# A hybrid layer on one core: the time mix's output product as three products of high parts and rests, with a new order of all engines' work

## The chip, the cores and the metric

The kernel runs on one core of a Trainium2 chip. A core has a matrix engine (TensorE, PE in the profile, with its weight loads as PEld), VectorE (DVE), ScalarE (ACT), GpSimd (POOL) and the queue of SyncE (SP), which issues most transfers. The metric is the device time of the program in microseconds (us). Lower is better.

## The reference, cut to what matters

The input x has 16 sequences of 512 tokens with 256 features. Four layers are added to it one after the other: a time mix with a channel mix, a layer of experts, a gated recurrence, and the same experts again. The part that the change touches is the time mix:

```
xn = layer_norm(x, ln1_w, ln1_b)
lx = time_shift(xn)
k = (xn * time_mix_k + lx * (1.0 - time_mix_k)) @ w_key      # v and r alike
out = wkv(w, time_first, k, v)                                # a recurrence over the tokens
x = x + out * sigmoid(r) @ w_output                           # this product changes
xn2 = layer_norm(x, ln2_w, ln2_b)                             # the channel mix follows
x = x + sigmoid(fr) * (square(relu(fk)) @ f_w_value)
```

and the last lines of the gated recurrence, `out = out @ W_out.T`, `rms = rsqrt(mean(out * out) + EPS)` and `out * rms * gamma`. The experts work on the first two sequences only (1024 tokens, two experts of eight for each token).

## The kernel before

One sequence is one run b of the time and channel mix (16 runs); the gated recurrence has runs p in an order of its own (`ORDER`), and the experts work on 20 tiles of 128 token rows in each of their two rounds (tiles 0 to 19 and 20 to 39). For each engine the order of the work is written out by hand: functions `turn_first`, `turn_0` to `turn_16` list calls such as `keys(5)` or `tile_up(8, 0)`, and each called helper waits on the semaphores of what it needs. Nothing is reordered when the program runs, so a helper that waits holds all that stands behind it on its engine. Turn i is about run i of the time mix, run i - 1 of the channel mix, and, from turn 4 on, a run of the recurrence and some tiles of the experts. The second round of the experts begins in turn 11 and needs the recurrence of the first two sequences, which are its runs 5 and 6.

A run of the time mix goes like this. Tokens are rows of a tile at first; TensorE transposes them (`transposes_in`), ScalarE writes the normed columns into `xn`, VectorE makes the differences and three mixed inputs. Keys, values and receptances are products of the weights `kw` with those inputs. They are split already: each float32 factor is written as a high part in the type float32r and the rest (also float32r), and `columns_split` adds three products, high by high, high by rest and rest by high. ScalarE makes a high part with a copy (`high_of_key`, L1240), VectorE the rest with a subtraction (`low_of_key`, L3372). Then VectorE runs the recurrence (`weights_ahead` to `numerators`), and `gated` ends it with the multiplication at L3480, which writes `mixed`, a half of the tile `dec`.

`outputs` on TensorE waits for that step, `mixture` "out", and multiplies `mixed` by `wo` with the helper `rows`: for each of four groups of 128 tokens and each of two groups of features one matmul with 128 columns of `mixed` as the stationary operand and 256 columns of `wo` as the moving one, in plain float32 (L2305). The trace shows a float32 matmul as two records and a float32r matmul as one. The result lies in the PSUM banks `rows_t`; `residual_mid` on VectorE (L3485) adds it to `y`, the second norm follows (`second_stats`, on GpSimd `norm2`), and `transposes_mid` on TensorE begins the channel mix. `second_differences` waits for the product too, since it writes over `dec`.

The tiles `timely` and `halves` lie at the same place in memory, one seen as float32 and one as float32r. `keys_out` on ScalarE (L1254) writes the keys into `kc`, a piece of `timely`, where `den`, the divisor of the run before, has been. The recurrence's own output product (`rec_products`, weights `gwo`) and the channel mix's receptance (`receptances`, weights `fwr`) use `rows` too, and stay as they are. Behind `rec_products` ScalarE squares the rows into a tile `square` that nobody reads, for their sum (L1364). At the start SyncE loads all weights; the ones that are split go to the tile `space`, which the recurrence uses later, and ScalarE and VectorE write the parts from there. `routing_masks` on GpSimd and `routing_spread`, `routing_counts`, `routing_products` and `slot_products` on TensorE, with small steps on VectorE between them, work out which token goes to which expert.

## Time and profile before

| | |
|---|---|
| median of 3 runs | 1272.68 us (1270.85 to 1278.52) |
| profiled execution | 1270.85 us |
| its span, first to last instruction | 1269.0 us |
| PE busy | 1173.5 us, 92% |
| DVE busy | 904.6 us, 71% |
| ACT busy | 769.0 us, 61% |
| POOL busy | 546.8 us, 43% |
| mean granted clock of TensorE | 0.975 |

Busy times are those of the profiled execution. Matmuls are pipelined, so the duration of a single matmul record is longer than the distance to the next one; what a group costs is read from the start of the group to the start of what follows. The granted clock is the share of TensorE's full speed that the chip allowed.

### The profile page before, as it was taken

How to read it: one execution, taken by the hardware profiler on the slowest of the kernel's cores; microseconds unless marked ns; L12 is line 12 of the kernel's file. 1: busy time of each engine (PE TensorE's matmuls, PEld its weight loads, DVE VectorE, ACT ScalarE, POOL GpSimd, SP SyncE). 2: the span in 40 equal slices, each digit the busy share in tenths (PEclk: the TensorE clock that was granted, in tenths of full speed). 3: DMA queues.
4: the chain of work that ended last, by engine and by line, in shares of the span. 5: the costliest groups of instructions: out<-in, count | busy, mean ns of one | idle time of the engine just before them, and what ended most of it. 6: DMA issues, size and time to landing. Idle time of an engine off the chain costs nothing. (4 is left out here: it accounts for less than half of the span.)

```text
span 1269.0 us, 17607 instructions
## 1 busy us (share of the span) xinstructions
PE 1173.5 (92%) x5992; PEld 968.4 (76%) x5992; DVE 904.6 (71%) x1539; ACT 769.0 (61%) x1164; POOL 546.8 (43%) x533
## 2 busy tenths in 40 slices
PE   4599999999999999999988999999999999998982
PEld 2487778888887877788876878878878788787871
DVE  7898887657666767776889898677686847544244
ACT  3464565754756657666757777568566575563533
POOL 3436742635034332362676546634453604323024
PEclk9699999999999999999999999999999999999996
DMA  7102156738556474574442134774667646756444
GB/s 207 31 18 50 18 146 202 209 96 221 181 160 189 115 209 130 162 216 157 109 91 59 26 67 140 205 203 134 161 163 201 170 149 179 216 162 140 130 151 123
DMA packets 115624, 180.64 MB, mean 142 GB/s; under 512 B 10312, under 2 KB 86736, under 8 KB 115536
## 3 DMA queue, kind: packets, MB, share of 16 engines
q1 hardware_dynamic: 94720, 124.46, 30.6%
q0 software_dynamic: 15056, 49.83, 19.9%
q10 hardware_dynamic: 5760, 5.25, 1.2%
q8 instruction: 48, 0.79, 0.3%
q14 instruction: 40, 0.33, 0.1%
HBM read 140.16 MB, written 16.27 MB: 123 GB/s over the span
## 5 line engine op out<-in xcount | busy, mean ns | idle before, releaser
L2394 PE MATMUL psum<-fwv,hid 128*128 128x256 f32 x1024 | 238.2, 382 | 3.8 <-ACT hid L1290 3.7
L2394 PEld LDWEIGHTS psum<-fwv,hid 128*128 128x128 f32 x1024 | 191.5, 191 | 31.1 <-ACT hid L1290 4.9
L803 POOL TENSOR_TENSOR rstd<-varis,half_neg 128x4 f32<-128x4 f32 x64 | 87.8, 1372 | 247.1 <-DVE varis L3316 180.1
L2435 PEld LDWEIGHTS psum<-xst,ew 128*128 128x128 f32 x1024 | 123.9, 193 | 5.8 <-ACT xst L1371 1.1
L2435 PE MATMUL psum<-xst,ew 128*128 128x128 f32 x1024 | 126.2, 277 | 1.1 <-DMA ew<-in_w 0.6
L2443 PE MATMUL psum<-ew,hidt 128*128 128x256 f32 x512 | 116.0, 380 | 1.3 <-ACT hidt L1384 1.3
L2443 PEld LDWEIGHTS psum<-ew,hidt 128*128 128x128 f32 x512 | 96.7, 190 | 15.3 <-ACT hidt L1384 1.9
L1286 ACT ACTIVATE hid<-psum 128x512 f32<-128x512 f32 x128 | 74.8, 594 | 54.9 <-PE psum L2298 34.8
L1384 ACT ACTIVATE hidt<-psum 128x512 f32<-128x512 f32 x80 | 47.9, 599 | 94.0 <-PE psum L2435 78.7
L927 POOL DMA_INDIRECT xs<-xf_rows,token_of_slot x40 | 52.8, 1320 | 119.4 <-PE psum L2423 102.7
L2298 PE MATMUL psum<-halves,kw_hi 128*128 128x512 f32 x360 | 103.7, 410 | 0.5 <-ACT timely L1259 0.4
L807 POOL TENSOR_SCALAR xhat<-rows_ring,negmean,rstd 128x256 f32<-128x256 f32 x104 | 97.4, 947 | 11.9 <-PE psum L2287 5.7
L2298 PE MATMUL psum<-xfk_hi,fwk_hi 128*128 128x512 f32 x256 | 90.0, 433 | 2.2 <-DVE parts L3337 1.5
L2298 PEld LDWEIGHTS psum<-halves,kw_hi 128*128 128x128 f32 x360 | 66.6, 191 | 19.0 <-issue 2.4
L2298 PE MATMUL psum<-xfk_hi,fwk_lo 128*128 128x512 f32 x256 | 81.0, 398 | 0.0
L2298 PE MATMUL psum<-parts,fwk_hi 128*128 128x512 f32 x256 | 80.6, 396 | 0.0
L1290 ACT ACTIVATE hid<-hid 128x512 f32<-128x512 f32 x128 | 78.1, 628 | 2.7 <-ACT ys L1392 1.6
L2298 PE MATMUL psum<-parts,gw_hi 128*128 128x512 f32 x256 | 72.2, 405 | 7.9 <-ACT space L1327 4.1
L2287 PE MATMUL psum<-ident,xhat 128*128 128x128 f32 x360 | 50.2, 285 | 30.9 <-POOL xhat L807 14.1
L3535 DVE SCALAR_TENSOR_TENSOR space<-space,vec 128x512 f32<-128x512 f32 x90 | 62.4, 760 | 14.3 <-ACT space L1307 14.3
L2287 PEld LDWEIGHTS psum<-ident,xhat 128*128 128x128 f32 x360 | 42.7, 147 | 38.0 <-issue 20.0
L3372 DVE TENSOR_TENSOR halves<-timely,halves 128x1024 fp32r<-128x1024 f32 x45 | 56.9, 1273 | 20.5 <-ACT halves L1248 7.8
(334 smaller groups left out, 2594.8 us busy)
## 6 DMA issues: line engine op xcount, KB each, us to landing
ew<-in_w SPq DMA_DIRECT2D x64, 1024.0 KB, 5.9
ew<-in_w SPq DMA_DIRECT2D x64, 512.0 KB, 5.1
rows_ring<-bias_rows POOLq DMA_DIRECT2D x28, 512.0 KB, 5.6
rows_ring<-in_x SPq DMA_DIRECT2D x14, 512.0 KB, 5.5
rows_ring<-y POOLq DMA_DIRECT2D x14, 512.0 KB, 6.1
out<-rows_ring SPq DMA_DIRECT2D x14, 512.0 KB, 7.1
rows_ring<-sf POOLq DMA_DIRECT2D x13, 512.0 KB, 6.3
rows_ring<-space POOLq DMA_DIRECT2D x12, 512.0 KB, 6.5
```

The source lines that it names most:

```text
L803: pool.tensor_tensor(dst, src, half_neg[:, 0:src.shape[1]], ALU.pow).then_inc(done, 1)
L807: pool.tensor_scalar(dst[:, c, :], src[:, c, :], negmean[n][:, c:c + 1], rstd[n][:, col0 + c:col0 + c + 1], ALU.add, ALU.mult).then_inc(st ...
L927: pool.indirect_dma_start(out=xs[n % 2][:], out_offset=None, in_=xf_rows, in_offset=bass.IndirectOffsetOnAxis(ap=token_of_slot[:, t:t + 1] ...
L1286: nc.scalar.activation(hid[:, j % NHID, :], ring[f"f{j}"], ACT.Relu).then_inc(relu.sem, 1)
L1290: nc.scalar.activation(hid[:, j % NHID, :], hid[:, j % NHID, :], ACT.Square).then_inc(sq.sem, 1)
L2287: last = nc.tensor.transpose(bank_t[:, c, k * P:(k + 1) * P], src[:, k, c * P:(c + 1) * P], ident[:])
L2298: last = nc.tensor.matmul(dst, w[a][:, c, m * P:(m + 1) * P], src[b][:, c, :], start=n == 0, stop=n == len(terms) - 1)
L2394: last = nc.tensor.matmul(rows4[:, k, :], hid[:, j % NHID, k * P:(k + 1) * P], fwv[:, j, :], start=j == 0 and k % 2 == 0, stop=j == FC - 1 ...
L2435: last = nc.tensor.matmul(bank_e[:, j * P:(j + 1) * P], ew1[:, c, at:at + P], xst[:, c, :], start=c == 0, stop=c == DC - 1)
L2443: last = nc.tensor.matmul(bank_e[:, 0:D], hidt[:, j, :], ew2[:, j, :], start=j == 0, stop=j == FC - 1)
L3372: nc.vector.tensor_tensor(parts[1], whole, parts[0].bitcast(F32), ALU.subtract).then_inc(lo.sem, 1)
L3535: nc.vector.scalar_tensor_tensor(s.cv[:, c, :], s.xc[:, c, j:j + T], col(f"conv{j}", c), s.cv[:, c, :], ALU.mult, ALU.add).then_inc(conv.s ...
```

## The change

The weight `wo` becomes two tiles, `wo[0]` (half of w_output as float32r) and `wo[1]` (the rest); w_output is loaded into a piece of `space` that is free then. After `gated`, ScalarE copies `mixed` to a float32r high part (`high_of_mixture`), which lies where `kc` and `den` are, and VectorE subtracts it from `mixed` in place (`low_of_mixture`). `outputs` waits for that rest and calls `rows_split`: for each group of 128 tokens six float32r matmuls instead of two float32 ones. Because the high part lies in `kc`'s place, `keys_out` now waits for the output product of the run before instead of for its `mixture`. The squares of the norm are written over the first 256 columns of the recurrence's states, which the product has read by then, and the tile `square` is gone. The calls in the turns of all five engines are in another order, and ScalarE's turns load the tables of its functions 94 times instead of 92. Cut to its core (in the turns only a few are shown, with the engine behind their first line):

```diff
...
-        wo = sb("wo", [P, DC, D])
+        wo = [sb(f"wo_{part}", [P, DC, D], F32R) for part in ("hi", "lo")]
...
+        with nc.sbuf_tensor("dec_parts", [P, 2, DC, T], F32R) as dec_parts:
+            mixed_parts = [carved(halves, 3 * DC * T, DC, T), dec_parts[:, 1]]
...
+        wo_whole = space[:, DC * FF + 5 * DC * D:DC * FF + 6 * DC * D].rearrange("p (c n) -> p c n", c=DC)
...
-        square = sb("square", [P, D])
...
+        mixture_hi = steps("mixture_hi", ["hi"], B)
+        mixture_lo = steps("mixture_lo", ["lo"], B)
+        wo_split = sem("wo_split")
...
-            for dst, src in ((wo, w_output), (fwr, f_w_recept), (fwv, f_w_value), (gwo, w_out_t)):
+            load_weight(wo_whole, w_output, weights_loaded)
+            for dst, src in ((fwr, f_w_recept), (fwv, f_w_value), (gwo, w_out_t)):
...
+            def high_of_mixture(b):
+                act.wait_ge(mixture.sem, mixture.count(b, "out"))
+                nc.scalar.activation(mixed_parts[0], mixed, ACT.Copy).then_inc(mixture_hi.sem, 1)
+
...
-                await_step(act, mixture, b - 1, "out")
+                await_step(act, proj, b - 1, "o")
...
-                    nc.scalar.activation(square[:], rows_t[:, c, :], ACT.Square, accum_out=ssq[:, c:c + 1])\
+                    nc.scalar.activation(rec_sets[set_of(p)].hs[:, 0, 0:D], rows_t[:, c, :], ACT.Square, accum_out=ssq[:, c:c + 1])\
...
+            def rows_split(dst, src, w, st):
+                terms = [(c, a, b) for a, b in ((0, 0), (1, 0), (0, 1)) for c in range(DC)]
+                for k in range(TC):
+                    for n, (c, a, b) in enumerate(terms):
+                        last = nc.tensor.matmul(dst[:, k, :], src[b][:, c, k * P:(k + 1) * P], w[a][:, c, :], start=n == 0,
+                                                stop=n == len(terms) - 1)
+                last.then_inc(st.sem, 1)
+
...
-                    pe.wait_ge(split_his, 3)
+                    pe.wait_ge(wo_split, 1)
...
-                pe.wait_ge(mixture.sem, mixture.count(b, "out"))
-                rows(rows_t, mixed, wo, DC, proj)
+                pe.wait_ge(mixture_lo.sem, mixture_lo.count(b, "lo"))
+                rows_split(rows_t, mixed_parts, wo, proj)
...
+
+            def split_wo_low():
+                dve.wait_ge(split_his, 3)
+                nc.vector.scalar_tensor_tensor(wo[1][:], wo_whole, 0.5, wo[0][:].bitcast(F32), ALU.mult, ALU.subtract)\
+                    .then_inc(wo_split, 1)
+
+            def low_of_mixture(b):
+                dve.wait_ge(mixture_hi.sem, mixture_hi.count(b, "hi"))
+                nc.vector.tensor_tensor(mixed_parts[1], mixed, mixed_parts[0].bitcast(F32), ALU.subtract).then_inc(mixture_lo.sem, 1)
...
-                nc.scalar.mul(wo[:], wo[:], 0.5).then_inc(split_his, 1)
+                nc.scalar.activation(wo[0][:], wo_whole, ACT.Copy, scale=0.5).then_inc(split_his, 1)
...
             def turn_0():   # TensorE
-                routing_spread()
                 freed(ev2, -1, 'e1')
                 freed(fr_out, -1, 's')
                 transposes_in(1)
                 freed(ev1, 1, 'e1')
                 outputs(0)
-                keys(1)
-                routing_counts()
-                routing_products()
                 freed(zsum, 0, 'z')
                 transposes_mid(0)
+                keys(1)
                 value_columns(1)
+                recept_columns(1)
+                channel_key(0, 0)
+                channel_key(0, 1)
...
             def turn_first():   # GpSimd
-                routing_masks()
                 norm1(0)
                 decay_power()
                 keep1(0)
+                norm1(1)
...
             def turn_0():   # GpSimd
-                norm1(1)
+                keep2(0)
                 norm2(0)
-                keep2(0)
+                routing_masks()
                 keep1(1)
...
             def turn_15():   # VectorE
-                weights_ahead(15)
                 gated_values(13)
-                surpluses(15)
-                low_of_receptance(15)
                 second_differences(14)
                 channel_mix_key(14)
+                low_of_receptance(15)
                 channel_mix_high(14)
+                channel_mix_receptance(14)
+                surpluses(15)
+                recur(12)
                 channel_mix_low(14)
-                channel_mix_receptance(14)
+                weights_decayed(15)
                 third_stats(13)
+                weights_now(15)
                 mean_square(12)
                 finish(12)
-                weights_now(15)
+                beta_sums(15)
+                decayed_values(15)
                 taps(13)
                 split_taps(13)
-                weights_decayed(15)
-                beta_sums(15)
-                denominators(15)
-                decayed_values(15)
                 alpha_sums(15)
                 weighted_values(15)
+                gated_input(13)
                 numerators(15)
+                denominators(15)
                 gated(15)
-                dve.wait_ge(mixture.sem, mixture.count(B - 1, 'out'))
-                nc.vector.memset(rec_sets[1].xc[:, :, 0:3], 0.0).then_inc(cols_made, 1)
+                low_of_mixture(15)
                 scales(13)
-                gated_input(13)
                 residual_mid(15)
+                second_stats(15)
...
```

The list of calls moves as a whole, so three places are shown as the engines' rows. The first is TensorE from its first instruction to the products of run 1 (`ident,xhat` is a transposition of tokens, `timely,space` the three unsplit products of run 0, `ew` with few columns the routing). Before:

```order
L2287 MATMUL psum<-ident,xhat 128x128 x8
L2292 MATMUL psum<-timely,space 128x512 x12
L2485 MATMUL psum<-ew 128x128 x2
L2486 MATMUL psum<-ew 128x1
L2287 MATMUL psum<-ident,xhat 128x128 x8
L2305 MATMUL psum<-wo,dec 128x256 x8
L2298 MATMUL psum<-halves,kw_hi 128x512 x4
```

and with the change:

```order
L2315 MATMUL psum<-ident,xhat 128x128 x8
L2320 MATMUL psum<-timely,space 128x512 x12
L2315 MATMUL psum<-ident,xhat 128x128 x8
L2341 MATMUL psum<-wo_hi,halves 128x256 x2
L2341 MATMUL psum<-wo_lo,halves 128x256 x2
L2341 MATMUL psum<-wo_hi,dec_parts 128x256 x2
...
L2315 MATMUL psum<-ident,xhat 128x128 x8
L2326 MATMUL psum<-halves,kw_hi 128x512 x4
```

The output product grows from 8 to 24 matmuls (the three rows stand four times, once for each group of tokens), the routing's first products are gone from here, and the transposition for run 0's channel mix now stands ahead of run 1's keys.

The second place is VectorE at the end of run 15 of the time mix. `dec<-timely,dec` ends `gated`, `y<-psum,y` is `residual_mid`, and the rows on `space` belong to the recurrence's run 13. Before:

```order
L3477 SCALAR_TENSOR_TENSOR timely<-timely 128x1024
L3480 TENSOR_TENSOR dec<-timely,dec 128x1024
L4274 MEMSET timely 128x2x3
L3554 TENSOR_TENSOR space<-space 128x1024
L3556 TENSOR_SCALAR space<-space 128x1024
L3678 SCALAR_TENSOR_TENSOR space<-space 128x1024
L3485 TENSOR_TENSOR y<-psum,y 128x1024
```

and with the change:

```order
L3522 SCALAR_TENSOR_TENSOR timely<-timely 128x1024
L3525 TENSOR_TENSOR dec<-timely,dec 128x1024
L3426 TENSOR_TENSOR dec_parts<-dec,halves 128x1024
L3599 TENSOR_TENSOR space<-space 128x1024
L3601 TENSOR_SCALAR space<-space 128x1024
L3530 TENSOR_TENSOR y<-psum,y 128x1024
```

The new subtraction stands right behind the multiplication whose result it needs, with ScalarE's copy between the two.

The third place is TensorE near the end: from the last part of run 14's channel mix (`fwv,hid`) to the transposition for the recurrence's run 14 (`ident,y`). Before:

```order
L2394 MATMUL psum<-fwv,hid 128x256 x8
L2435 MATMUL psum<-xst,ew 128x128 x8
L2305 MATMUL psum<-gwo,space 128x256 x8
L2298 MATMUL psum<-xfk_hi,fwk_hi 128x512 x2
...
L2423 MATMUL psum<-ident,xs 128x128 x2
L2287 MATMUL psum<-ident,y 128x128 x8
```

and with the change:

```order
L2430 MATMUL psum<-fwv,hid 128x256 x8
L2315 MATMUL psum<-ident,xhat 128x128 x8
L2471 MATMUL psum<-xst,ew 128x128 x8
L2333 MATMUL psum<-gwo,space 128x256 x8
L2471 MATMUL psum<-xst,ew 128x128 x8
...
L2459 MATMUL psum<-ident,xs 128x128 x2
L2430 MATMUL psum<-fwv,hid 128x256 x4
L2315 MATMUL psum<-ident,y 128x128 x8
```

Between the two ends there now stand another transposition (`transposes_mid(15)`), one more half tile of the experts (`xst,ew`) and one more part of the channel mix (`fwv,hid` x4), and four key products (`xfk_hi,fwk_hi` with their two companions) instead of five.

## Rows read from the trace of the kernel before

**Rows 1.** Stretches of the span, all engines: length, then busy time of each
```profile
core 0: us, PE busy (x) PEld busy (x) DVE busy (x) ACT busy (x) POOL busy (x), PEclk, DMA share, GB/s
40.00:60.00 20.00, 13.44 (x49) 11.15 (x50) 16.36 (x38) 6.92 (x8) 3.61 (x3) 0.67 0.05 10
60.00:200.00 140.00, 133.76 (x626) 112.30 (x626) 121.81 (x209) 80.69 (x110) 70.86 (x62) 0.97 0.30 75
200.00:600.00 400.00, 393.64 (x2132) 326.42 (x2132) 276.26 (x449) 251.80 (x377) 153.63 (x157) 1.00 0.60 169
600.00:760.00 160.00, 147.48 (x679) 122.00 (x678) 141.42 (x256) 111.83 (x169) 100.58 (x85) 0.98 0.33 74
760.00:1160.00 400.00, 393.27 (x2105) 324.01 (x2104) 273.11 (x437) 255.83 (x404) 168.09 (x155) 1.00 0.62 174
1160.00:1218.00 58.00, 53.41 (x272) 46.73 (x271) 19.84 (x42) 27.41 (x48) 11.11 (x15) 0.97 0.40 108
```
**Rows 2.** Timeline of PE around 604 us: start, us, line, operation, count
```profile
603.34 1.09 PE L2298 MATMUL psum<-halves,kw_hi 128*128 128x512 f32 x4
604.26 0.62 PE L2298 MATMUL psum<-halves,kw_lo 128*128 128x512 f32 x2
604.72 1.95 PE L2435 MATMUL psum<-xst,ew 128*128 128x128 f32 x16
606.51 3.62 PE L2305 MATMUL psum<-gwo,space 128*128 128x256 f32 x16
609.96 1.95 PE L2435 MATMUL psum<-xst,ew 128*128 128x128 f32 x16
```
**Rows 3.** Timelines of PE and, last, DVE at the start
```profile
41.57 1.97 PE L2287 MATMUL psum<-ident,xhat 128*128 128x128 f32 x8 [11.89 <-POOL xhat L807]
45.08 6.63 PE L2305 MATMUL psum<-wo,dec 128*128 128x256 f32 x16 [1.54 <-ACT xn L1220]
51.35 1.27 PE L2298 MATMUL psum<-halves,kw_hi 128*128 128x512 f32 x4
54.30 0.28 PE L2490 MATMUL psum<-ew 128*128 128x1 f32 x2
59.80 1.94 PE L2287 MATMUL psum<-ident,xhat 128*128 128x128 f32 x8 [0.81 <-DVE xhat L3508]
...
41.21 1.38 DVE L3480 TENSOR_TENSOR dec<-timely,dec 128x1024 f32<-128x1024 f32 x1
```
**Rows 4.** Groups of VectorE and ScalarE: count | busy, mean ns | idle before
```profile
L3372 DVE TENSOR_TENSOR halves<-timely,halves 128x1024 fp32r<-128x1024 f32 x45 | 56.9, 1273 | 20.5 <-ACT halves L1248 7.8 <-ACT halves L1240 7.2 <-ACT halves L1244 5.4
L1240 ACT ACTIVATE halves<-timely 128x1024 fp32r<-128x1024 f32 x15 | 15.8, 1052 | 9.2 <-DVE timely L3329 9.2
```
**Rows 5.** Timelines of DVE and PE, runs 3, 11 and 15
```profile
194.47 1.22 DVE L3480 TENSOR_TENSOR dec<-timely,dec 128x1024 f32<-128x1024 f32 x1
195.84 3.69 PE L2305 MATMUL psum<-wo,dec 128*128 128x256 f32 x16
...
791.79 3.69 PE L2305 MATMUL psum<-wo,dec 128*128 128x256 f32 x16 [0.17 <-DVE dec L3480]
...
1127.71 1.22 DVE L3480 TENSOR_TENSOR dec<-timely,dec 128x1024 f32<-128x1024 f32 x1
1130.26 3.62 PE L2305 MATMUL psum<-wo,dec 128*128 128x256 f32 x16
```
**Rows 6.** GpSimd: its norm rows, durations min/median/max, and four of them at 31.81
```profile
L807 POOL TENSOR_SCALAR xhat<-rows_ring,negmean,rstd x104: 543/554/3556, 80.0 to 1217.7; 128x256 f32<-128x256 f32 x104
...
31.81 9.71 POOL L807 TENSOR_SCALAR xhat<-xf,negmean,rstd 128x256 f32<-128x256 f32 x4 [0.20 <-issue]
```
**Rows 7.** Timeline of PE at the end of the dense part
```profile
1150.28 1.95 PE L2435 MATMUL psum<-xst,ew 128*128 128x128 f32 x16
...
1165.94 0.38 PE L2423 MATMUL psum<-ident,xs 128*128 128x128 f32 x2
1170.90 1.94 PE L2287 MATMUL psum<-ident,y 128*128 128x128 f32 x8 [4.59 <-DVE space L3578]
```

More of the change, by code:

```diff
@@ L1610, in turn_5 @@
[L1610 to L1623 removed]
+                relu_of(4, 5)
@@ L1762, in turn_8 @@
-            def turn_8():
                 rows_back(15)
                 tile_columns(16)
+            def turn_8():
+                norm_mid(7)
+                high_of_value(8)
+                high_of_receptance(8)
+                keys_out(8)
                 values_out(8)
+                nc.scalar.preload_act_table_set(GELU_TANH)
+                receptances_out(8)
                 rows_of_two(16, 0)
+                sums_of_squares(3)
+                relu_of(7, 0)
                 rows_of_two(16, 1)
+                square_of(7, 0)
@@ L1805, in turn_8 @@
                 gelu_of(18, 0)
+                high_of_key(9)
+                high_of_receptance(9)
                 gelu_of(18, 1)
+                rows_back(18)
                 relu_of(7, 5)
-                nc.scalar.preload_act_table_set(LOG_EXP)
-                root_of(4)
-                rows_back(18)
+                relu_of(7, 6)
+                high_of_value(9)
+                tile_columns(19)
+                keys_out(9)
+                gelu_of(19, 0)
+                square_of(7, 4)
@@ L2724, in turn_5 @@
+                channel_key(4, 7, 1)
+                tile_up(8, 1)
                 channel_value(4, 4)
-                keys(6)
-                channel_value(4, 5)
-                tile_down(9)
+                tile_down(8)
                 freed(zsum, 5, 'z')
                 transposes_mid(5)
-                tile_in(10)
+                tile_in(9)
+                keys(6)
+                value_columns(6)
+                tile_up(9, 0)
+                channel_value(4, 5)
                 channel_value(4, 6)
@@ L4124, in turn_11 @@
                 mixed_receptance(12)
+                gated_values(10)
+                residual_mid(11)
+                low_of_key(12)
                 second_stats(11)
```

1969 lines of the change are left out of this document (991 added, 978 removed).

## The prediction, made before the changed kernel was run

> **What bounds the kernel now.** I read the stretches of the span first. From 200 to 600 us and from 760 to 1160 us TensorE is busy for 393.6 and 393.3 of 400 us while VectorE is busy for 276 and 273 [rows 1]: there each microsecond of matrix work is one of the program. From 60 to 200 us TensorE idles 6.2 of 140 us with VectorE 87% busy (121.8), and from 600 to 760 us it idles 12.5 of 160 us with VectorE 88% busy (141.4) [rows 1]: there both engines are nearly full, and the chain through VectorE has a say. Second comes the timeline of TensorE, for what a matmul costs: the reader is to take start to start. 16 records of plain float32 with 256 moving columns take 609.96 - 606.51 = 3.45 us, 216 ns each; 16 records with 128 moving columns take 606.51 - 604.72 = 1.79 us, 112 ns each; six float32r matmuls with 512 columns take 604.72 - 603.34 = 1.38 us, 230 ns each [rows 2]. Third, the start and the end, where TensorE waits: for 11.89 us before 41.57 [rows 3], and for 4.59 us before 1170.90 [rows 7]. Fourth, how far the output product stands behind the multiplication that feeds it. In run 3 the one ends at 195.69 and the other starts at 195.84, in run 15 the distance is 1.33 us, and in run 11 the product waited 0.17 us [rows 5].
>
> **Matrix work of the product.** In each of 15 runs the 16 records of 3.45 us are replaced by 24 float32r ones with 256 moving columns. No such row exists. The nearest from below is 112 ns: a record with a weight load of the same size that streams half as long [rows 2]. If the time of a float32r matmul goes with its columns, 256 of them take half of 230 ns, 115; if the 14 ns by which it exceeds the float32 record (230 - 216) are a fixed price of each matmul, it is 216 / 2 + 14 = 122 ns. I take 118, between these two. 24 x 118 = 2.83 us, 0.62 less than 3.45, and 15 x 0.62 = 9.3 us. Run 0 goes at a granted clock of 0.67 and its product takes 51.35 - 45.08 = 6.27 us [rows 1, 3]; in the same ratio (2.83 / 3.45) it is 1.1 us less. Term: -10.4. Its ends: 112 ns give 15 x 0.76 + 1.4 = -12.8; 122 ns give 15 x 0.52 + 0.9 = -8.7; the upper end of what the rows allow is 230 ns, if the weight load and not the streaming sets the pace of float32r, and it is a rival below. The Trainium skill, page "TensorE: Matmul & The Clock Gate", section "Back-to-back issue gap", has columns / 2.4 + 2.5 ns, 109 ns for 256 columns; this term by it would be -14.0. For the 512 columns of float32r here it gives 216 ns where the row has 230, so the row decides.
>
> **VectorE's new subtraction.** One for each run, 16 in all, at 1273 ns for the same form and size [rows 4], 20.4 us, and 0.7 us once for the weight's rest. Where TensorE is the bound, VectorE's idle third covers it: nothing. In runs 1 to 3 and in 9 and 10, which fall into the two stretches where VectorE is 87 to 88% busy [rows 1], there is little cover. There I give back the matrix saving, 5 x 0.62 = 3.1 us, and count half of the new work, 5 x 1.27 / 2 = 3.2. Term: +6.3. Ends: 0 (the saving is kept and the idle eighth covers it) and 3.1 + 6.4 = +9.5. GpSimd may feel it as well: four norm rows of GpSimd took 9.71 us at 31.81 where one is 554 ns in the median and up to 3556 [rows 6], beside VectorE's work. The Trainium skill, "GPSIMD Engine Reference", section "1. Specifications", says that GpSimd shares its SBUF interface with VectorE instructions that have two SBUF inputs; the new subtraction is one, and by that rule each would hold GpSimd for its length, which speaks against the change: 16 x 1.27 = 20.4 us of GpSimd's time would go by it. GpSimd is busy 153.6 of 400 us and 100.6 of 160 [rows 1], so it has room for delays of that size, and I add nothing.
>
> **ScalarE's copy and two more table loads.** 16 x 1.05 us at the row of the same copy [rows 4], under 20 us with the tables, on an engine busy 252 and 256 of 400 us in the dense stretches [rows 1]. Cover: its idle third. Nothing, and at most what the next term has. The later release of `keys_out` costs nothing either, since it also waits for the keys' own product, which stands behind the output product on TensorE. The squares go to another place at the same size; w_output is one transfer of the same size to another place.
>
> **The wait for the rest.** From the multiplication to the product there are now ScalarE's copy, 1.05 us, VectorE's subtraction, 1.27, and handoffs, about 2.5 us. At the old distances runs 3, 10 and 11 (0.15 us each) would be short by 2.35 and runs 1 and 15 (about 1.3) by 1.2: 3 x 2.35 + 2 x 1.2 = 9.5 us [rows 5] (they show 3, 11 and 15 of the sixteen pairs in the timelines). Behind the waiting product stand the experts' tiles and, through `residual_mid`, the second norm. The new order was made with this step in it: in VectorE's rows of run 15 nothing stands between the multiplication and the subtraction. I take +1, with ends 0 and +9.5.
>
> **The start.** The norm rows of run 1 and their transposition move ahead, so the 11.89 us of waiting go; but the output product of run 0 still ends a chain on VectorE that ends at 42.59 (41.21 + 1.38) and now has copy and subtraction behind it: it starts at 42.59 + 2.5 = 45.1, as now at 45.08 [rows 3]. It is 1.1 us shorter (counted above). The dense part begins with run 0's second transposition, 59.80 now, and some 2 us earlier then, since the routing's small steps are gone from VectorE in front of it. But the keys' products of run 1, 54.30 - 51.35 = 2.95 us, and the routing's own matmuls, about 2 us, which filled the gap, go behind it. 2.95 + 2 - 2 - 1.1 = +1.9, and I take +1.5. Ends: -1 and +4.
>
> **The end.** In front of the transposition that waited 4.59 us stood 1165.94 - 1150.28 = 15.7 us of other work [rows 7]. Now it is one transposition (8 records of 112 ns, 0.9 us), one half tile (1.79) and one part of the channel mix (8 records of 216 ns, 1.7) more, and one key product (six of 230 ns, 1.4) less: 3.0 us more cover for the same chain. I take -2; ends -4.6 and +2. Behind it the recurrence's last run is the same work in the same order.
>
> **Sum:** -10.4 + 6.3 + 1 + 1.5 - 2 = -3.6, from 1270.85 for the profiled execution (span 1269.0 and 1.85 around it) to 1267.2. The median of before, 1272.68, is 1.8 us above that execution. I say 1267. One per cent, 12.7 us, is about what this measurement can tell from no change: the bounds are 1260.0 and 1285.4. The likeliest case's own range is 1261 to 1275, chance 0.50.
>
> **Rivals.** (1) The saving arrives whole and the new order closes gaps. TensorE idled 36 us between 60 and 1218 us [rows 1] (6.2 + 6.4 + 12.5 + 6.7 + 4.6); if a quarter of that goes as well, it is -10.4 - 9 = -19, 1252. For it: the lists were redone on all engines. Against: the idle time is largest where VectorE is full, and VectorE gets 21 us more. Chance 0.30. (2) The rest comes too late. The high part and the rest are two new steps in a row, and where the product stands closer than 2.5 us behind the multiplication TensorE stands still, in the two stretches where VectorE is full also for the steps behind it: -10.4 + 9.5 + 9.5 + 4 = +12.6, 1283. It decides as soon as the distances of rows 5 are kept in the runs named. Chance 0.14. (3) Float32r is paced by its weight loads: then 24 x 230 ns = 5.52 us instead of 3.45, 15 x 2.07 = +31.1 and run 0 +3.8; nothing is left to give back, so with the new work, the wait, the start and the end (3.2 + 1 + 1.5 - 2) it is 1270.85 + 38.6 = 1309. The point from which the product itself loses is 3.45 / 24 = 144 ns. For it: every float32r row that there is has 230 ns. Against: a float32 record with its load of 128 columns comes each 112 ns [rows 2]. Chance 0.06.
>
> **Range and chances.** Low end: -12.8 with no loss elsewhere and part of rival 1, 1252. High end: rival 2 with the product at 122 ns, 1286. What is outside is rival 3 and the tails, under 2 in 10. Faster by over 1%: most of rival 1 and a little of the main case, 0.30. Slower by over 1%: rival 3 and near half of rival 2, 0.12. Within: 0.58.
>
> **What would show it.** The output product from start to the next start: 2.83 us (2.7 to 2.95), not 5.5. TensorE's wait in front of it, by release from the subtraction: under 2 us in sum, against 9.5 in rival 2. Idle time of TensorE from 600 to 760 us: above 12.5 us here, below it in rival 1. TensorE's dense part begins near 57.7 us, and the wait in front of the last-but-one transposition of the recurrence is under 3 us. Wrong it would be if the new order moved TensorE's idle time by more than 10 us either way, which no row of the kernel before can tell.

## The result, and the profile after

The changed kernel takes 1255.03 us (median of 4 runs, 1253.22 to 1259.97), the kernel before, timed beside it, 1273.82 (1270.85 to 1278.52): a ratio of 0.9855, 95% interval 0.9813 to 0.9897, some 18.8 us less. Run again with the experiments it took 1253.01 against 1274.79, a ratio of 0.9838 (0.9818 to 0.9859). The forecast was 1267 in a range of 1252 to 1286, with 0.58 on "within 1%" and 0.30 on faster. The time is in the range, but the kernel is faster by over 1%, which had 0.30: it is the time of rival 1, outside the main case's own 1261 to 1275.

The page of the changed kernel, busy time of each engine (before: 1173.5, 904.6, 769.0 and 546.8 us in a span of 1269.0):

```profile
span 1252.9 us, 17899 instructions
PE 1159.5 (93%) x6120; PEld 963.1 (77%) x6120; DVE 927.4 (74%) x1556; ACT 786.5 (63%) x1182; POOL 586.9 (47%) x533
```

The stretches of the span, with the same columns as [rows 1]; the bounds are moved with the work:

```profile
40.00:60.00 20.00, 6.04 (x31) 5.90 (x32) 18.04 (x29) 4.01 (x4) 7.83 (x17) 0.59 0.14 26
60.00:200.00 140.00, 135.75 (x681) 115.24 (x679) 123.86 (x219) 90.60 (x120) 85.63 (x67) 0.98 0.28 69
200.00:600.00 400.00, 396.17 (x2209) 330.11 (x2208) 290.93 (x465) 259.49 (x387) 176.99 (x161) 1.00 0.62 175
600.00:745.00 145.00, 132.59 (x612) 109.81 (x611) 129.64 (x223) 100.17 (x152) 92.34 (x78) 0.95 0.30 67
745.00:1140.00 395.00, 389.00 (x2123) 322.11 (x2123) 280.15 (x461) 262.95 (x407) 178.43 (x155) 1.00 0.62 173
1140.00:1202.00 62.00, 61.22 (x328) 53.60 (x328) 28.41 (x52) 31.93 (x59) 12.32 (x14) 1.00 0.51 136
1202.00:1252.90 50.90, 22.97 (x109) 18.45 (x107) 24.56 (x41) 16.90 (x34) 20.88 (x22) 0.77 0.48 143
```

Read length minus busy time of PE. From 60 us to the end of the dense part TensorE idles 4.3, 3.8, 12.4, 6.0 and 0.8 us, 27.3 together, where [rows 1] give 36.4. VectorE is 23 us busier, and TensorE still waits less. From 600 to 760 us it idles 12.4 us, as before (12.5). The prediction had wanted more in its main case and less in rival 1, so this sign decides nothing.

The timeline of TensorE at run 1's output product and the next group, then at run 0's product and the start of the dense part:

```profile
92.88 0.58 PE L2341 MATMUL psum<-wo_hi,halves 128*128 128x256 f32 x2
93.30 0.40 PE L2341 MATMUL psum<-wo_lo,halves 128*128 128x256 f32 x2
...
95.66 0.40 PE L2341 MATMUL psum<-wo_hi,dec_parts 128*128 128x256 f32 x2
95.90 1.46 PE L2430 MATMUL psum<-fwv,hid 128*128 128x256 f32 x6
...
44.98 0.77 PE L2341 MATMUL psum<-wo_hi,halves 128*128 128x256 f32 x2 [15.00 <-DVE dec_parts L3426]
45.97 0.63 PE L2341 MATMUL psum<-wo_hi,dec_parts 128*128 128x256 f32 x2
...
49.16 0.40 PE L2341 MATMUL psum<-wo_hi,dec_parts 128*128 128x256 f32 x2
58.53 1.94 PE L2315 MATMUL psum<-ident,xhat 128*128 128x128 f32 x8 [8.97 <-DVE xhat L3553]
```

From the second pair of records to the next group there are 22 records in 95.90 - 93.30 = 2.60 us, 118 ns each: the price that was taken. The first pair takes 93.30 - 92.88 = 0.42 us, though, so the whole product lasts 3.02 us here. In the 14 runs in which the next group follows at once it lasts 2.90 to 3.04 us, 2.92 in the median, instead of the 2.83 that were forecast. The dense part begins at 58.53 instead of 59.80. And the end of the dense part, against the wait of 4.59 us in [rows 7]:

```profile
1156.83 0.38 PE L2459 MATMUL psum<-ident,xs 128*128 128x128 f32 x2
1157.05 1.89 PE L2430 MATMUL psum<-fwv,hid 128*128 128x256 f32 x8
1158.78 1.04 PE L2315 MATMUL psum<-ident,y 128*128 128x128 f32 x8
```

The wait is gone. Behind the last tile of the experts the program takes 48.0 us where it took 50.0 (1252.9 - 1204.9 and 1269.0 - 1219.0). The matmuls there are the same and run at a higher granted clock (the gates' products take 5.7 us at 1.00 instead of 7.3 at 0.79), and the new order alone has 50.1, so these 2 us are not the order's.

What TensorE waited for in the changed kernel (the waiting line, the step that released it, sum in us, times, longest), and the new steps' groups (count | busy, mean ns | idle before and what ended it):

```profile
PE psum L2333 <- DVE space L3608: 21.2, 5, 11.7
PE psum L2315 <- DVE xhat L3553: 18.7, 2, 9.8
PE psum L2341 <- DVE dec_parts L3426: 16.2, 4, 15.0
PE psum L2315 <- POOL xhat L813: 3.6, 2, 2.5
...
L3426 DVE TENSOR_TENSOR dec_parts<-dec,halves 128x1024 fp32r<-128x1024 f32 x16 | 19.8, 1238 | 18.5 <-ACT halves L1258 18.5
L1258 ACT ACTIVATE halves<-dec 128x1024 fp32r<-128x1024 f32 x16 | 16.9, 1056 | 8.2 <-DVE dec L3525 7.8 <-ACT ys L1402 0.4
```

The wait for the rest is 16.2 us, but 15.0 of them are the start, where TensorE has no other work; in the other runs of the time mix it is 1.2. The groups show another wait: VectorE stands idle 18.5 us in front of its subtraction, because ScalarE's copy comes late, up to 5.51 us late:

```profile
411.25 1.23 DVE L3525 TENSOR_TENSOR dec<-timely,dec 128x1024 f32<-128x1024 f32 x1
417.98 1.23 DVE L3426 TENSOR_TENSOR dec_parts<-dec,halves 128x1024 fp32r<-128x1024 f32 x1 [5.51 <-ACT halves L1258]
```

So the result looks like rival 1: the whole saving and 9 us of idle time (36.4 - 27.3). The experiments say otherwise.

### The profile page after: what moved, and what is told of

Read it like the earlier page. It is cut to its first block, busy times and chain, and to the rows that moved or that the text cites. A ratio compares the mean times of both kernels' runs of the same rounds, so it can differ in the third digit from the quotient of the medians.

```text
span 1252.9 us, 17899 instructions
## 1 busy us (share of the span) xinstructions
PE 1159.5 (93%) x6120; PEld 963.1 (77%) x6120; DVE 927.4 (74%) x1556; ACT 786.5 (63%) x1182; POOL 586.9 (47%) x533
## 4 chain that ended last, share of the span: by engine, by line
PE 24%; DVE 9%; issue 7%; ACT 4%; POOL 4%; DMA 2%; DVEq 0%; POOLq 0%; ACTq 0%
PE psum L2326 8%; PE psum L2333 4%; PE psum L2430 4%; PE psum L2471 2%; PE psum L2479 2%; DVE space L3580 1%; PE psum L2493 1%; PE psum L2511 1%; PE psum L2315 1%; DVE stats L3345 1%; POOL xhat L813 1%; DMA rows_ring<-sf 1%; POOL rstd L809 1%; DVE timely L3365 1%; DVE dec L3377 1%
## 5 line engine op out<-in xcount | busy, mean ns | idle before, releaser
L809 POOL TENSOR_TENSOR rstd<-varis,half_neg 128x4 f32<-128x4 f32 x64 | 99.2, 1550 | 205.7 <-DVE varis L3352 142.1
L813 POOL TENSOR_SCALAR xhat<-rows_ring,negmean,rstd 128x256 f32<-128x256 f32 x104 | 116.7, 1132 | 10.5 <-POOL rstd L809 5.8
L2333 PE MATMUL psum<-gwo,space 128*128 128x256 f32 x240 | 62.9, 422 | 21.2 <-DVE space L3608 21.2
L2333 PEld LDWEIGHTS psum<-gwo,space 128*128 128x128 f32 x240 | 50.7, 215 | 33.1 <-issue 21.1
L1226 ACT ACTIVATE xn<-psum,vec 128x512 f32<-128x512 f32 x64 | 46.2, 775 | 45.2 <-PE psum L2315 42.3
```

The source lines that it names most:

```text
L809: pool.tensor_tensor(dst, src, half_neg[:, 0:src.shape[1]], ALU.pow).then_inc(done, 1)
L813: pool.tensor_scalar(dst[:, c, :], src[:, c, :], negmean[n][:, c:c + 1], rstd[n][:, col0 + c:col0 + c + 1], ALU.add, ALU.mult).then_inc(st ...
L2333: last = nc.tensor.matmul(dst[:, k, :], src[:, c, k * P:(k + 1) * P], w[:, c, :], start=c == 0, stop=c == chunks - 1)
```

## The experiments

Twelve runs in three groups of four, each timed beside the kernel before, whose medians in the groups were 1272.56, 1274.79 and 1274.44. Each ratio is to the kernel before of its own group. A difference between two ratios carries the noise of both: worked out from their 95% intervals it is good to about 4 us either way, and to 6 against the first measurement of the changed kernel. In the diffs, lines are against the changed kernel unless it says otherwise.

**The new order alone.** The old product, its weight and its waits, with the changed kernel's calls in their new order:

```diff
-                pe.wait_ge(mixture_lo.sem, mixture_lo.count(b, "lo"))
-                rows_split(rows_t, mixed_parts, wo, proj)
+                pe.wait_ge(mixture.sem, mixture.count(b, "out"))
+                rows(rows_t, mixed, wo, DC, proj)
...
-                high_of_mixture(0)     # and the other 15, and low_of_mixture
```

> The changed kernel's order of all engines with the old float32 product (no high part, no rest, wo in float32, keys_out waits for the mixture again). Theory A, two gains: the product's 24 records at 118 ns save 0.6 us in each run (10.4 us in all) and the new order by itself takes some 9 us of TensorE's idle time away; then this kernel is 8 to 10 us slower than the changed one, 1263 to 1266 us, and clearly faster than the kernel before. Theory B, the order only hides the new steps of ScalarE and VectorE: then the order alone brings nothing, and this kernel is at 1270 to 1275 us. Theory C, the order brings all and the product nothing: 1253 to 1257 us.

Measured: 1252.95 us, ratio 0.9848 (0.9825 to 0.9870). That is Theory C: the order alone brings 19.6 us, as much as the whole change, and the product with its steps nothing on top. (The squares keep their new place in this kernel. The third splice below has that place too and takes the time of before, so the place is worth nothing.) Its stretches:

```profile
60.00:200.00 140.00, 136.85 (x666) 116.54 (x665) 121.02 (x218) 87.10 (x116) 82.42 (x66) 0.99 0.28 69
200.00:600.00 400.00, 396.62 (x2147) 328.67 (x2146) 283.04 (x456) 253.84 (x380) 177.13 (x160) 1.00 0.62 175
600.00:745.00 145.00, 134.17 (x607) 111.03 (x607) 129.45 (x232) 100.21 (x152) 93.85 (x81) 0.96 0.30 67
745.00:1140.00 395.00, 391.32 (x2096) 324.39 (x2096) 277.30 (x450) 259.73 (x404) 178.30 (x157) 1.00 0.62 174
1140.00:1200.00 60.00, 60.00 (x318) 52.74 (x317) 24.33 (x48) 30.22 (x59) 12.42 (x16) 1.00 0.49 139
```

TensorE idles 3.2, 3.4, 10.8, 3.7 and 0 us, 21.0 together instead of 36.4: 15.4 us of the 17.9 by which the two profiled spans differ (1269.0 and 1251.1). The tail behind the last tile of the experts is as long as before (50.1 against 50.0 us). The waits that went are those of [rows 7] (4.59) and many small ones. TensorE's waits for GpSimd's norm rows (`xhat`) come to 2.7 us in 2 places where they were 14.1 in 5 (11.9 of these stood at the start, where 12.6 on the multiplication now stand instead).

**The new form in the old order.** The kernel before with the new product, the copy put behind `norm_in` of the next run, the subtraction behind the multiplication or the next `first_differences`:

```diff
...
                 norm_in(6)
+                high_of_mixture(5)
...
                 gated(5)
+                low_of_mixture(5)
```

> The new product in the order of the kernel before: ScalarE's copy stands right behind norm_in of the next run (or behind inverse, whichever is later), VectorE's subtraction right behind the next run's first differences where these follow gated, else right behind gated. Theory A: the product's 10.4 us come, and of the waits for the rest (short distances in runs 1, 3, 10, 11, 15) 4 to 10 us are lost: 1264 to 1270 us. Theory B: product and waits cancel and VectorE's 20 us cost more: 1272 to 1280 us. Theory C would have it at 1273 us, as before.

Measured: 1306.58 us, ratio 1.0259 (1.0231 to 1.0288), worse than all three theories. TensorE waited for the rest itself only 9.5 us, 4.0 of it at the start, so rival 2 is a small part of it. More comes by way of ScalarE, as the waits of TensorE and, last, of ScalarE show:

```profile
PE psum L2339 <- DVE dec_parts L3424: 9.5, 5, 4.0
PE psum L2324 <- ACT space L1337: 8.9, 5, 3.1
PE psum L2477 <- ACT hidt L1394: 6.9, 3, 5.6
PE psum L2324 <- ACT hid L1296: 6.6, 2, 5.8
PE psum L2428 <- ACT hid L1300: 5.6, 2, 3.6
...
ACT halves L1258 <- DVE dec L3523: 25.2, 9, 6.6
```

The copy that I had placed holds ScalarE for 25.2 us until the multiplication is done, and steps of ScalarE (`space`, `hidt`, `hid`) are late for TensorE: 28.0 us in the four rows, of which the kernel before has 4.1 for `space` and 3.7 for `hid` among its larger ones. That they are late because they queue behind the copy is read from the waits; no run shows it, and the second try below, where ScalarE's wait for the multiplication is 12.2 us instead of 25.2, was slower still.

**The third product left out.** High part of the mixture by the weight's rest is not computed, 16 records instead of 24:

```diff
-                terms = [(c, a, b) for a, b in ((0, 0), (1, 0), (0, 1)) for c in range(DC)]
+                terms = [(c, a, b) for a, b in ((0, 0), (0, 1)) for c in range(DC)]
```

> The changed kernel without the third product (high part by the weight's rest is left out): 16 instead of 24 records in each output product, 8 x 118 ns = 0.94 us less of TensorE in each of 16 runs, 15.1 us, and nothing else moved. If TensorE is the bound in all stages: 1240 us. If five runs lie where VectorE holds (my term of the prediction gave the saving of runs 1 to 3, 9 and 10 back): 11 x 0.94 = 10.3 us, 1245 us. If the order was fitted to the length of the product and gaps open: above 1247 us.

Measured: 1247.36 us, ratio 0.9798 (0.9778 to 0.9819). 8 records of 118 ns in 16 runs are 15.1 us of matrix work, and the ratio is 0.57 and 0.40 points below the two of the changed kernel, 7.3 and 5.1 us: 0.3 to 0.5 us for each. That is the third case, just above 1247 us, by a margin that the noise does not carry; 1245 is as possible. The trace speaks for gaps that open: measured as in the table of the next section, the matrix work is 12 to 14 us less than in the two profiles of the changed kernel, and TensorE idles 33.7 us where it idled 27.9 and 27.8.

**More work on VectorE.** Three small statistics instructions of an idle weight stand right behind each subtraction of runs 1 to 15; VectorE's busy time rises from 927.4 to 941.0 us:

```diff
+                if b:
...
+                    for c in range(3):
+                        nc.vector.bn_stats(spare[:, c, :], fwv[:, c, :]).then_inc(spare_made, 1)
```

> The changed kernel with more VectorE work right behind the new subtraction in runs 1 to 15: three statistics of 256 columns of a constant tile, some 1.2 us, 18 us in all, which nobody reads. My prediction charged half of the new VectorE work in runs 1 to 3, 9 and 10 (about 3 us) and nothing elsewhere: 1258 us. If VectorE has room everywhere: 1255 us. If VectorE's chains set the pace more often than its busy share tells: 1262 us or more.

Measured: 1260.85 us, ratio 0.9897 (0.9875 to 0.9919), 0.42 and 0.59 points above the two of the changed kernel: 5.3 and 7.5 us for 13.6 us of VectorE, 0.4 to 0.55 each. The smaller of the two is within its noise, the larger is not. Measured in the same way, TensorE idles 32.4 us here, 4.5 more than in the changed kernel. The idle quarter of VectorE does not hide the load, in a part of the program where TensorE is 98% busy (27.3 us idle of 1142).

**The changed kernel once more**, as the base of the next three.

> The changed kernel once more, on the same chip as the three other runs, as the base of their differences. Both theories: 1254 to 1256 us, a ratio of 0.985 to the kernel before.

Measured: 1253.01 us, ratio 0.9838 (0.9818 to 0.9859).

**The steps without the form.** Copy, subtraction and the wait for it are kept, the product is the old one:

```diff
-                rows_split(rows_t, mixed_parts, wo, proj)
+                rows(rows_t, mixed, wo, DC, proj)
...
-                nc.vector.tensor_tensor(mixed_parts[1], mixed, mixed_parts[0].bitcast(F32), ALU.subtract)
+                nc.vector.tensor_tensor(mixed_parts[0], mixed, mixed_parts[0].bitcast(F32), ALU.subtract)
```

> The new order with ScalarE's copy, VectorE's subtraction and the wait for it kept, but the product itself is the old one, 16 records of plain float32 on the multiplication's result (the subtraction's result goes to the copy's place and is read by nobody; the keys' output waits for it). Theory H (the new steps cost about half of what the cheaper product saves, and each side counts at 0.3 to 0.5 us per us): 1258 to 1262 us, 3 to 6 above the changed kernel, and 6 to 9 above the new order alone. Rival I (the new steps are hidden in the new order, and the new product simply brings nothing): 1252 to 1255, like the new order alone.

Measured: 1258.61 us, ratio 0.9874 (0.9853 to 0.9894), 5.6 above the changed kernel, or 4.6 by the ratios, just outside the noise: Theory H. Against the new order alone it is 3.3 us slower (0.26 points of the ratio), which is within the noise.

**The form without the steps.** 24 float32r records, no copy, no subtraction:

```diff
-                rows_split(rows_t, mixed_parts, wo, proj)
+                rows_split(rows_t, (mixed_parts[1], mixed_parts[1]), wo, proj)
...
-                nc.vector.tensor_tensor(mixed, den[:], num, ALU.mult).then_inc(mixture.sem, 1)
+                nc.vector.tensor_tensor(mixed_parts[1], den[:], num, ALU.mult).then_inc(mixture.sem, 1)
```

> The new order with 24 float32r records in the product, but without the copy and without the subtraction: the multiplication writes its result as float32r at once, and it stands for both parts (so the rest of the mixture is left out, and one of the three products is wrong). Theory H: the saving of 10.4 us counts at about half and nothing is paid, 1246 to 1249 us, 6 to 9 below the changed kernel. Rival I: the product brings nothing even without its steps, 1252 to 1255. Rival J (the saving arrives in full, since no step is new): 1241 to 1244.

Measured: 1244.84 us, ratio 0.9777 (0.9754 to 0.9800), below Theory H's range and near rival J's. Against the new order alone this is 0.71 points, 9.0 us, of the 10.4 that the sum had for it. Here the saving arrives nearly whole, within the noise.

**Splices of the two orders**, all with the old product. In the first, every engine takes the calls of the new order up to turn 4, and then those that are left in the old order; the second is its mirror image; the third has the old order up to turn 12.

> The old product; every engine takes the new order up to turn 4 and what is then left in the old order. The new order alone was 12.2 us ahead at run 5's output product, 9.2 at run 9's, 16.0 at run 14's and 18.0 at the last tile. Theory K (the gain is made where it shows, in pieces that don't depend on each other): the first piece stays, 1259 to 1263 us, and run 5's output product is 10 to 13 us earlier than before. Rival L (a lead made early is given back, because the old order's later work waits for other things, such as the experts' transfers and the recurrence's first runs): 1267 to 1272.

Measured: 1288.64 us, ratio 1.0116 (1.0097 to 1.0135), worse than both theories. Run 4's product stands 0.7 us ahead of before, run 5's 12.4 behind, and from there the distance stays between 12.4 and 15.7 to the end. What TensorE waited for between 289 and 372 us, at the seam:

```profile
PE psum L2478 <- DMA ew<-in_w: 6.5, 1, 6.5
PE psum L2311 <- DVE halves L3393: 3.3, 1, 3.3
```

The transfer of an expert's weights comes 6.5 us late there and the keys' parts 3.3. So this run prices its seam and not its pieces: inconclusive on Theory K, except that the old order behind the seam kept its old length.

> The old product; every engine takes the old order up to turn 4 and what is then left in the new order, the mirror image of the run that lost 13 us at its seam. Theory K: the part behind the seam is 6 to 9 us shorter than before, the total between 1264 and 1272 us by what the seam costs, and the distance from run 5's output product to the end shrinks by 5 us or more against the kernel before. Rival P: the seam alone decides again, 1280 or more.

Measured: 1259.66 us, ratio 0.9880 (0.9861 to 0.9899). Theory K, below its 1264 to 1272: the part from turn 5 on brings 14.8 us, three quarters of the order's gain. Its second sign failed, though. In the profiled execution (1258.5 us against 1269.0) run 5's output product is 6.6 us earlier than before and the distance from it to the end only 3.9 us shorter, where 5 or more were expected: most of what this profile shows is gained right behind the seam.

> The old product; every engine takes the old order up to turn 12 and what is then left in the new order. In the new order alone the distance from run 12's output product to the end is 9 to 11 us shorter than before. Theory K (the last part of the new order is shorter by itself): 1262 to 1267 us. Rival P (the new order's end is short only because its middle left the work in another state, or the seam costs what the end brings): 1271 or more, with waits of TensorE near 880 us.

Measured: 1272.76 us, ratio 0.9991 (0.9975 to 1.0007): the last turns of the new order bring nothing by themselves. The 4.59 us in front of the last-but-one transposition are gone there too, but run 12's product is 5.6 us late and run 13's 14.0 at the seam, and the end then recovers most of it (the last tile 4.9 behind). Rival P, with the same reserve as above: seam and end can't be told apart.

**The form alone in the old order.**

> The old order of all engines with 24 float32r records in the product, without the copy and without the subtraction (the multiplication writes its result as float32r and it stands for both parts; the rest of the mixture is left out). In the new order the same edit brought 9.0 us against the old product (a ratio of 0.9777 against 0.9848). Theory M (the form of the product is worth about as much in either order, and what the earlier run with the whole form in the old order lost, 34 us, came from where I put the two steps): 1262 to 1267 us. Rival N (the old order is tuned so closely to its own lengths that even a shorter product disturbs it): 1270 or more.

Measured: 1274.02 us, ratio 1.0004 (0.9990 to 1.0018). Rival N: the same edit that brings 9.0 us in the new order brings nothing in the old. Its trace shows places where it is given back. Run 3's product is 3.4 us ahead of before and run 5's 3.8, run 6's 1.6 ahead, run 9's 4.0 behind. The timeline of TensorE there, of this kernel and then of the kernel before:

```profile
473.83 0.60 PE L2484 MATMUL psum<-ident,hid_rows 128*128 128x128 f32 x4
478.58 1.09 PE L2297 MATMUL psum<-ident,xhat 128*128 128x128 f32 x8 [4.15 <-DVE space L3605]
```

```profile
475.31 0.60 PE L2466 MATMUL psum<-ident,hid_rows 128*128 128x128 f32 x4
478.24 1.07 PE L2287 MATMUL psum<-ident,xhat 128*128 128x128 f32 x8 [2.32 <-DVE space L3578]
```

TensorE arrives 1.5 us earlier and starts 0.3 us later, since VectorE's step of the recurrence was done no sooner. And there is a second loss, in the granted clock, again of this kernel and then of the one before:

```profile
480.00:500.00 20.00, 19.96 (x112) 15.60 (x108) 15.45 (x17) 13.83 (x19) 6.00 (x7) 0.93 0.53 152
640.00:660.00 20.00, 15.63 (x73) 13.22 (x73) 15.92 (x25) 12.31 (x19) 17.21 (x16) 0.83 0.17 46
700.00:720.00 20.00, 17.57 (x76) 14.91 (x77) 17.12 (x26) 14.80 (x21) 10.07 (x11) 0.83 0.28 53
```

```profile
480.00:500.00 20.00, 19.21 (x117) 15.72 (x114) 15.70 (x18) 14.24 (x20) 6.17 (x7) 1.00 0.51 151
640.00:660.00 20.00, 17.74 (x80) 14.88 (x80) 18.57 (x23) 13.72 (x21) 16.56 (x14) 0.91 0.20 56
700.00:720.00 20.00, 19.95 (x88) 16.65 (x87) 18.58 (x21) 15.99 (x22) 9.03 (x7) 0.93 0.11 21
```

Behind the longer waits the engine runs part of the time at 1.2 instead of 2.4 GHz.

**The form in the old order, the copy moved** to where its input was ready in the trace of the first try:

> The whole new form in the old order again, with ScalarE's copy moved in twelve of the sixteen runs by 1 to 8 calls, to about where its input came in the trace of the first try (which had ScalarE wait 25.2 us for the multiplication in nine runs and the copy 4 to 7 us late in four others). Theory M: most of the loss was this placement, 1272 to 1285 us against 1307. Rival O (two more steps in the chain cost the old order that much wherever the copy stands, since VectorE's work behind them is late): 1298 or more.

Measured: 1325.01 us, ratio 1.0401 (1.0379 to 1.0424), 18 worse than before the move. Rival O, and a miss of mine: TensorE now waited 24.6 us for the rest in 8 places, since every step behind the moved copies shifted as well. What the first trace said about where the copies should stand did not hold once they had been moved.

Of the kernels that compute the whole product none beats the new order alone (0.9848) and the changed kernel (0.9855 and 0.9838), and these two can't be told apart. The two with lower times, 0.9777 and 0.9798, leave a part of the product out.

## Why the prediction was right in its range and wrong in its reasons

The dense stretch, from 60 us to the last tile of the experts, splits into three parts when the stretches are read in steps of 20 us: TensorE's idle time, the time lost to the lower clock (1 minus the granted clock, times the length), and the rest, which is matrix work at full clock (good to 2 or 3 us).

| kernel | length | idle | clock | rest |
|---|---|---|---|---|
| before | 1159.0 | 37.0 | 9.4 | 1112.6 |
| new order alone | 1141.0 | 21.6 | 7.2 | 1112.2 |
| new order, steps, old product | 1147.2 | 23.2 | 9.2 | 1114.8 |
| new order, new product, no steps | 1132.4 | 23.7 | 4.6 | 1104.1 |
| changed kernel | 1144.9 | 27.9 | 11.4 | 1105.6 |
| changed kernel, second profile | 1141.0 | 27.8 | 6.4 | 1106.8 |
| old order, new product, no steps | 1163.6 | 44.3 | 15.4 | 1103.9 |
| old order, whole form | 1202.6 | 73.0 | 30.2 | 1099.4 |

**Matrix work: right in size.** 118 ns for a record was taken and 118 measured, but not for the first pair of a product (0.42 us instead of 0.24). With 2.92 us in the median a run saves 0.53 us instead of 0.62, 8.0 us in 15 runs where 9.3 were forecast. Run 0's product takes 4.4 us instead of 6.3, 1.9 us less and not 1.1, because the granted clock rose in its middle. All kernels with the new product have 6 to 13 us less in the last column. Rival 3 (paced by weight loads, 230 ns) is out. The Trainium skill, "TensorE: Matmul & The Clock Gate", section "Back-to-back issue gap", has a formula for the gap of an isolated matmul that gives 109 ns for 256 columns. The 118 ns of the trace do not agree with it.

**What the saving is worth: wrong as a rule.** The prediction said that in the dense stretches "each microsecond of matrix work is one of the program". It is that only if the rest of the program can follow. With the copy and the subtraction in place the cheaper product brings 5.6 us (1258.61 to 1253.01); without them 9.0; in the old order 0. In the new order the sum's own figure, 10.4 less the 3.1 given back, stands between the first two; it has no place for the third.

**VectorE's subtraction: the step that was mis-sized.** I charged 3.2 us, for five runs, and for the other ten nothing under "VectorE's idle third covers it". The load added on VectorE cost 0.4 to 0.55 us per us with TensorE 98% busy around it: 5.3 to 7.5 us for 13.6, where my rule (half, in five runs of fifteen) gives 2.3. The two steps together cost 8.2 us with the new product (1244.84 to 1253.01), against the 3.2 + 1 that the sum had for them and their wait. With the old product they cost 3.3, which the runs can't tell from nothing. By the lengths in the table the steps cost 8.6 us with the new product and 6.2 with the old one; the whole times show less because the two kernels without the steps had an end that was 2 us longer. A part of that is ScalarE's copy, charged at zero: it is late in 7 runs of the time mix and VectorE stands still for 18.5 us. How the 8.2 divide between copy, subtraction and the later release of the keys' output was not measured.

**GpSimd: right to add nothing, though the rule holds.** The Trainium skill, "GPSIMD Engine Reference", section "1. Specifications", lets GpSimd contend with VectorE instructions that have two SBUF inputs, and by it I had counted 20.4 us of GpSimd's time for the subtractions. The trace of the changed kernel agrees with the rule: four norm rows take 2.18 us, 0.55 each, with VectorE idle beside nearly all of them, and 6.25 us, the first two of them 2.6 each, beside VectorE's instructions with two inputs. Over the whole trace the 86 norm rows that overlap no VectorE instruction take 0.55 us in the mean, and 110 that overlap one with two SBUF inputs take 1.52.

```profile
208.19 2.18 POOL L813 TENSOR_SCALAR xhat<-y,negmean,rstd 128x256 f32<-128x256 f32 x4 [0.30 <-POOL rstd L809]
214.65 1.23 DVE L3377 TENSOR_TENSOR dec<-xn 128x1024 f32<-128x1024 f32 x1 [6.34 <-ACT xn L1226]
...
397.90 6.25 POOL L813 TENSOR_SCALAR xhat<-rows_ring,negmean,rstd 128x256 f32<-128x256 f32 x4 [0.30 <-POOL rstd L809]
397.98 2.33 DVE L3506 TENSOR_TENSOR_SCAN timely<-dec 128x512 f32<-128x512 f32 x2
```

The new subtractions hardly meet such rows: 4 of GpSimd's 244 norm rows overlap one. So GpSimd is busy for 586.1 us in the new order alone and for 586.9 with the subtractions, and the 20.4 us don't show. The 40 us more than before (546.8) come with the order: the same 104 rows of `xhat` take 947 ns in the mean before, 1148 in the new order alone and 1132 in the changed kernel.

**The wait for the rest: right.** 1 us was taken, 1.2 measured outside the start. **The start:** taken at +1.5, ends -1 and +4. The dense part begins 1.3 us earlier (2 were expected), and 2.8 us earlier in the new order alone (57.05), which has no steps behind the multiplication. The work that was moved into it is as expected, but no run isolates the term. **The end:** taken at -2, ends -4.6 and +2; the wait of 4.59 is gone, the lower end, and the spliced order does not show it to be a gain by itself.

**The new order: the step that failed.** Outside the start and the end the sum has nothing for it, and the prediction put it as what would make it wrong: "if the new order moved TensorE's idle time by more than 10 us either way". The order alone moved it by 15.4 us, and it is the whole result, -19.6, where the sum has 1.5 - 2 = -0.5 for it. The steps then put 6 us of idle time back, so the changed kernel by itself shows -9.1, and rival 1's parts (-10.4 for the product and -9 for idle time) seem to fit. What the runs show is -19.6 for the order, about -9 for the product and about +8 for its steps. That the time fell into the range was luck. The main case had -3.1 for the product with its steps (-10.4 + 6.3 + 1) and -0.5 for the order, and the runs show about 0 and -19.6; the range reached down to 1252 for another reason, the full saving with a quarter of the idle time beside it. The sum also starts from the profiled execution, 1270.85. From the median, 1272.68, it would have said 1269, and rival 1 1253 to 1254. Read as the prediction could have read it: 46 of 1159 us (37.0 and 9.4, the first row of the table) are lost in idle time and clock, and that is what an order can move. I allowed it a quarter of the idle time at a chance of 0.30 alone.

**What stays open.** Three quarters of the order's gain, by one splice with a seam in it, lie in what stands from turn 5 on. Which moved calls they are is not shown, and the splices can't show it, since a seam costs up to 13 us. Whether the whole form could be placed in the old order at less than +2.6% isn't shown either; both tries were placed by hand.

## What to carry to other kernels

Price the order apart from the operations: run the new order with the old operation and the old order with the new one, before a gain is put down to either. In a program whose engines all run in a fixed order, a microsecond saved on the bounding engine is worth between nothing and one, by whether the waits of the next stage move with it; here 0 in the old order, 0.5 and 0.9 in the new. And an engine that is 70% busy need not hide new steps in a chain that the bounding engine comes back to: here a microsecond of them cost about half a microsecond.

## What the hardware showed that was not expected

In these traces the granted clock fell behind some of TensorE's waits of 2 to 4 us and not behind others. The same program, the changed kernel, in its two profiled executions, TensorE's timeline and the stretch of the first:

```profile
674.33 6.38 PE L2333 MATMUL psum<-gwo,space 128*128 128x256 f32 x16 [3.43 <-DVE space L3608]
680.54 1.89 PE L2430 MATMUL psum<-fwv,hid 128*128 128x256 f32 x8
...
660.00:680.00 20.00, 15.80 (x62) 12.59 (x61) 19.68 (x35) 9.61 (x14) 17.89 (x12) 0.83 0.15 27
```

```profile
674.41 3.69 PE L2333 MATMUL psum<-gwo,space 128*128 128x256 f32 x16 [3.45 <-DVE space L3608]
677.94 1.89 PE L2430 MATMUL psum<-fwv,hid 128*128 128x256 f32 x8
```

After the same wait (3.43 and 3.45 us) the same 16 records take 680.54 - 674.33 = 6.21 us in the one and 3.53 in the other, where the granted clock of that stretch is 0.83 and 1.00. So this wait cost its length and, in one execution, 2.7 us more. A wait of 2.49 us before 153.92, in the first profile, was followed by the lower clock too (0.52 from 154.0 to 157.4 us). In the table the lower clock, wherever it came from, is 4.6 to 15.4 us of a kernel's time, and 30.2 in the one with most idle time. It also makes executions of one program differ: the two profiles of the changed kernel differ by 3.7 us in the profiled time (1254.81 and 1251.12) and by 5.0 us in this column.
